# Gathered edges of a graph network: one product per chunk of 128 edges, over 64 destination columns at a fixed place

## The chip, the cores and the metric

One core of one Trainium2 chip runs the whole kernel in one launch. The metric is the device time of one execution in microseconds (us), as the median of the runs shown. Engines are named as the profile names them: PE is TensorE's matmul, PEld its weight load, DVE is VectorE, ACT ScalarE, POOL GpSimd, SP SyncE.

## What is computed

A graph of N = 6250 nodes with D = 128 features and E = 106250 edges, sorted by destination, goes through 14 aggregations one after the other: two SAGE layers, one GCN, two more GCN products, and three layers of three hops each. Each aggregation has the form

```
agg[n] = sum over edges e with dst[e] == n of scale(e) * x[src[e]]        # segment_sum(x[src], dst)
h      = f(agg @ W + x @ W' + b), then a layer norm and a residual in some of them
```

The first five aggregations (the GCN scalings are done on the nodes) sum rows without an edge's weight; the nine hops multiply each row by `edge_weight[e]`.

## The kernel before, in words

Nodes are cut into 49 tiles of 128. An aggregation is a stage `a` (0 to 13), and a stage computes its destination tiles in two ways at once.

**Dense part.** For the later tiles a matrix of edge counts (stages 0 to 4) or edge weights (stages 5 to 13) lies in HBM. SP loads it in units into `room` (6 slots), and `sweep` (L1021) multiplies each of the 49 source tiles with a piece of 512 columns (four destination tiles) into `pwide`.

**Sparse part.** The first 12 tiles (6 pairs; `EARLY`, `FIRST`) or 18 tiles (9 pairs; `LATE`) are done from gathered rows. A pair has `CHP` = 36 chunks of 128 consecutive edges. POOL gathers the source rows of a chunk with one indirect DMA into one of 36 slots of `ring_f` (L628). DVE builds a one-hot of 128 edges by 128 destinations in `hot`, 27 buffers (`one_hot`, L1532 to L1538). PE multiplies the gathered rows by the one-hot into `pstep` (`edges`, L1034 to L1055; the product is L1051). The first 16 chunks of a pair hold only edges of its first tile and those from the 20th on only edges of the second, but chunks 16 to 18 may hold both. So a pair has `STP` = 39 steps for 36 chunks: `step_of` gives for each step the chunk, the side and whether the chunk is new, and the three middle chunks are multiplied twice. `last_step` says which step frees a slot.

Steps go in batches of `HB` = 3 with one semaphore count each (`hot_built`, `batch_done`). All matmuls are f32, and each shows as two weight loads and two passes in the profile. The order on PE is written out by the host: a stage has so many beats, a beat holds the products of 11 of the `sum(dense) * 49` tile pairs (some 2.75 wide products), then the posts (transposes and products with weight matrices) that are due, then the batches that `beat_of` puts there. `lead` beats at the start of a stage (6, 9 in `LATE`, 90 in stage 0) and `trail` beats at its end (8, 4, 2) have no batch.

POOL starts the gathers of stage `a` when all rows of stage `a - 1` are in the table (`rows_out`). Gather `c` waits until the slot's previous chunk has been used (`batch_done`) and, every other chunk, until PE has come to a unit of the sweep (`pace`, at most `AHEAD_UNITS` ahead). In stages 1 to 4 POOL also writes the edge weights of the late matrix with 536 indirect DMAs (`scatter`, L591), spread between the gathers, with some 40 behind the last one.

DVE's work after a group (`post`) is put between the one-hots of the batch that `due` gives, `FH` = 5 batches behind.

**Front.** Before stage 0, DVE sums repeated edges for the scatter lists (`summed`, `place`), counts where tiles begin, decides if the input fits the fast way (`flag`, L1326 to L1336, then `v_flag`), and gives POOL the places of the chunks (`off_i`, L1322, then `off_ready`). Each engine waits for `v_flag` and loads it before its fast part. POOL's fast part first fetches the edge records of the chunks with 21 indirect DMAs (L604: 9 for destinations, 9 for weights, 3 for sources), then scatters 360 and 300 columns of counts (L591), of which each lap waits for the one before to land, and then gathers for stage 0. The counts matrix is zeroed before by ACT's DMA queue (`counts<-zz`); the first scatter waits for 35 of these. DVE's `tables` waits for the 21 fetches, and a walk over 49 tiles of 21 chunks sums the degrees (PE L901, DVE L1370).

Of the kernel before, what the change touches and what calls it, by code (L numbers as in the profile page):

```python
# [10 lines left out]
P = 128  # L11
# [29 lines left out]
STP = 39  # L41
# [3 lines left out]
RB = 3  # L45
HOTS = 27
HB = 3
LEAD, TRAIL = 6, 8
# [9 lines left out]
assert STP % HB == 0 and HOTS % HB == 0 and 2 * MIX + 4 == CHP and CHP + 3 == STP  # L58
KINDS = [0, 1, 2, 3, 4] + ["hop1", "hop2", "hop3"] * LAYERS


def last_step(c):
    return c if c < MIX else 2 * c - MIX + 1 if c < MIX + 3 else c + 3


def step_of(i):
    if i < MIX:
        return i, 0, True
    if i < MIX + 6:
        return MIX + (i - MIX) // 2, (i - MIX) % 2, (i - MIX) % 2 == 0  # L70
    return i - 3, 1, True
# [76 lines left out]
RBLOCKS = -(-((TILES + 1) // 2) // RB)  # L148
WINDOW = 40
# [5 lines left out]
assert SPAN % HB == 0 and SPAN <= HOTS and SPAN >= MIX + 3  # L155
# [3 lines left out]
def pace(a, c):  # L159
    p, (pair, slot) = SPLITS[a], divmod(c, CHP)  # L160
    first = slot if slot < MIX else MIX + 2 * (slot - MIX) if slot < MIX + 3 else slot + 3
    m = p.beat_of((pair * STP + first) // HB) * p.mm // p.beats
# [34 lines left out]
def program(nc, A, out):  # L197
    ctx = ExitStack()
    with ctx:
# [50 lines left out]
        f_dst = sb("f_dst", [P, TILES, SPAN])  # L250
        f_dst_flat = f_dst[:, :, :].rearrange("p t c -> p (t c)")
# [16 lines left out]
        hot = sb("hot", [P, HOTS, P])  # L268
# [89 lines left out]
        v_group = sem("v_group")  # L358
        lanes_in, p_flag, v_flag, lanes_ready, x_copied, kept = names(
# [212 lines left out]
        def _(pool):  # L572
# [8 lines left out]

            def scatter(which, i):
# [12 lines left out]
            def fast():  # L595
                pool.wait_ge(off_ready, 1)
                pool.wait_ge(e_out, 96)
                for k in range(RBLOCKS):
                    n = min(RB * CHP, (PAIRS - 1 - k * RB) * CHP + MIX + 3)
                    for rows_, pad in ((rows_d.bitcast(I32), e_dst), (rows_w, e_wgt), (rows_s.bitcast(I32), e_src)):  # L600
                        if pad is e_src and k * RB >= MOST:
                            continue
                        runs = pad.rearrange("(e a) -> e a", a=1)
                        pool.indirect_dma_start(out=rows_[0:n, k, :], out_offset=None, in_=runs[:, :],  # L604
                                                in_offset=bass.IndirectOffsetOnAxis(ap=off_i[0:n, k:k + 1], axis=0)
                                                ).then_inc(fast_rows, 16)
# [7 lines left out]
                for a, p in enumerate(SPLITS):  # L614
# [253 lines left out]
        def _(pe):  # L868
# [6 lines left out]
            pe.matmul(pstep[1][0:1, 0:1], same[:, 1:2], ones[:, 0:1], start=False, stop=True).then_inc(p_flag, 1)  # L875
            pe.wait_ge(in_w, 16 * (10 + len(ROWS) + 3))
# [5 lines left out]
            def tables_and_degrees():  # L882
                pe.wait_ge(fast_rows, (2 * RBLOCKS + 3) * 16)
# [144 lines left out]
            def selves(a, bank, first, w):  # L1028
                for i in range(w):
                    own = x_of(a)[:, first + i, :]  # L1030
                    ins = pe.matmul(bank[:, i * P:(i + 1) * P], own, ident[:, :], start=False, stop=i == w - 1)
# [786 lines left out]
```

## Time and profile before

| what | value |
| --- | --- |
| median of 3 runs (lowest, highest) | 7283.2 us (7281.24, 7289.38) |
| span of the profiled execution | 7281.5 us |
| PE busy | 6698.5 us, 92% |
| PE weight loads busy | 3984.2 us, 55% |
| POOL busy | 4999.4 us, 69% |
| DVE busy | 2253.5 us, 31% |
| ACT busy | 363.8 us, 5% |
| DMA | 2043.46 MB, mean 281 GB/s |

The page gives the span of the profiled execution and no other time of it. The span is within 0.3 us of the lowest of the three runs. Busy time is the union of the instructions of an engine; POOL's busy time is the part of each indirect DMA in which it writes descriptors, and 0.30 us of issue lie between two of them.

### The profile page before, as it was taken

What the parts mean: (1) busy time and instruction counts of PE and PEld (TensorE: products, weight loads), DVE (VectorE), ACT (ScalarE), POOL (GpSimd) and SP (SyncE); (2) the same over time, 40 slices, a digit from 0 to 9 for tenths busy, and PEclk for the clock granted to TensorE, in tenths of its full rate; (3) what the DMA queues carried; (4) which work ended last, traced back from release to release, by engine and by line L of the source; (5) the groups of instructions that cost most, each with busy time, mean ns of one, the idle gap of its engine ahead of it and who ended that gap; (6) DMA issues with size and microseconds to landing.
All of it is one profiled execution on the core that took longest, in us unless ns stands there. A gap on an engine that the chain in (4) does not pass through costs nothing.

```text
span 7281.5 us, 76418 instructions
## 1 busy us (share of the span) xinstructions
PE 6698.5 (92%) x25545; PEld 3984.2 (55%) x25546; DVE 2253.5 (31%) x8529; ACT 363.8 (5%) x1003; POOL 4999.4 (69%) x5223
## 2 busy tenths in 40 slices
PE   0599749899999999999999999999999999999998
PEld 0599325555555555555555555556555555655555
DVE  8444602222112111222323234322222432322244
ACT  0000000000001000000000000000000000000000
POOL 0677777676666776776767767676776767767676
PEclk9999979999999999999999999999999999999999
DMA  9977738788787887887888888888888888888887
GB/s 363 353 284 292 242 118 281 245 291 295 266 278 258 291 297 276 303 303 258 283 286 284 276 300 279 279 277 283 290 279 293 280 284 278 275 292 285 304 288 236
DMA packets 593113, 2043.46 MB, mean 281 GB/s; under 512 B 135284, under 2 KB 328599, under 8 KB 418780
## 3 DMA queue, kind: packets, MB, share of 16 engines
q1 hardware_dynamic: 309150, 1605.95, 62.3%
q0 software_dynamic: 167184, 263.90, 12.1%
q10 hardware_dynamic: 116428, 169.16, 6.4%
q8 instruction: 193, 3.16, 0.2%
q14 instruction: 158, 1.29, 0.1%
HBM read 1768.09 MB, written 271.72 MB: 280 GB/s over the span
## 4 chain that ended last, share of the span: by engine, by line
PE 66%; DMA 14%; POOL 11%; issue 8%; DVE 0%; POOLq 0%; SPq 0%; ACT 0%; ACTq 0%; DVEq 0%
PE pwide L1021 52%; PE pstep L1051 11%; DMA ring_f<-table,f_src 6%; POOL ring_f L628 5%; DMA counts<-lane_val,lane_idx 4%; POOL counts L591 4%; DMA counts<-zz 3%; POOL weights L591 1%; PE pwide L1105 1%; DMA weights<-lane_val,lane_idx 1%; DMA ring_f<-in_x,f_src 0%; PE pwide L1104 0%; PE pwide L1067 0%; DMA room<-weights 0%; PE pwide L1071 0%
## 5 line engine op out<-in xcount | busy, mean ns | idle before, releaser
L628 POOL DMA_INDIRECT ring_f<-table,f_src x3780 | 3596.2, 951 | 1603.0 <-issue 974.4
L1021 PE MATMUL pwide<-room,hcur 128*128 128x512 f32 (+2 forms) x6076 | 2616.8, 573 | 112.8 <-DMA room<-counts 112.8
L1021 PE MATMUL pwide<-room,acc 128*128 128x512 f32 (+2 forms) x5880 | 2555.4, 575 | 15.2 <-DMA room<-weights 13.5
L1021 PEld LDWEIGHTS pwide<-room,hcur 128*128 128x128 f32 x6076 | 1079.1, 191 | 1106.3 <-issue 1063.3
L1051 PEld LDWEIGHTS pstep<-hot,ring_f 128*128 128x128 f32 x8658 | 1192.2, 192 | 737.9 <-issue 544.9
L1021 PEld LDWEIGHTS pwide<-room,acc 128*128 128x128 f32 x5880 | 1045.7, 191 | 959.6 <-issue 908.4
L1051 PE MATMUL pstep<-hot,ring_f 128*128 128x128 f32 x8658 | 1244.8, 277 | 128.6 <-DMA ring_f<-table,f_src 111.7
L1537 DVE TENSOR_SCALAR hot<-iota,f_dst,f_wgt 128x128 f32<-128x128 f32 x3159 | 892.2, 362 | 1478.0 <-PE pstep L1051 1471.7
L591 POOL DMA_INDIRECT counts<-lane_val,lane_idx x660 | 648.9, 983 | 220.7 <-issue 182.9
L591 POOL DMA_INDIRECT weights<-lane_val,lane_idx x536 | 525.5, 980 | 164.0 <-issue 152.1
L1536 DVE TENSOR_SCALAR hot<-iota,f_dst 128x128 f32<-128x128 f32 x1170 | 260.2, 301 | 811.1 <-PE pstep L1051 806.8
L901 PE MATMUL pstep<-acc,hot 128*128 x2058 | 446.7, 353 | 40.2 <-DVE deg_sums L1375 40.2
L901 PEld LDWEIGHTS pstep<-acc,hot 128*128 128x128 f32 x2058 | 442.7, 332 | 44.2 <-issue 44.2
L1558 DVE SCALAR_TENSOR_TENSOR xres<-pwide,dinv,xres 128x128 f32<-128x128 f32 x294 | 83.3, 344 | 845.3 <-PE pwide L1105 697.4
L628 POOL DMA_INDIRECT ring_f<-in_x,f_src x216 | 204.7, 948 | 65.8 <-issue 60.0
L721 ACT ACTIVATE zz<-pwide 128x512 f32<-128x512 f32 x122 | 70.3, 576 | 3398.3 <-PE pwide L1021 2623.5
L1558 DVE SCALAR_TENSOR_TENSOR zz<-pwide,dinv,xres 128x128 f32<-128x128 f32 x196 | 55.5, 344 | 541.3 <-PE pwide L1105 336.9
L1370 DVE TENSOR_SCALAR hot<-iota,f_dst 128x128 f32<-128x128 f32 x1029 | 208.6, 294 | 2.8
L1105 PEld LDWEIGHTS pwide<-w,zz 128*128 128x128 f32 x882 | 122.4, 192 | 35.6 <-issue 30.6
L604 POOL DMA_INDIRECT ring_f<-e_dst,off_i x9 | 9.3, 1039 | 192.2 <-issue 191.9
L1105 PE MATMUL pwide<-w,zz 128*128 128x128 f32 x882 | 135.2, 275 | 0.6 <-ACT zz L721 0.6
L1558 DVE SCALAR_TENSOR_TENSOR zz<-pwide,rcnt,rows 128x128 f32<-128x128 f32 x49 | 13.9, 344 | 318.6 <-PE pwide L1096 318.6
(261 smaller groups left out, 1674.9 us busy)
## 6 DMA issues: line engine op xcount, KB each, us to landing
room<-weights SPq DMA_DIRECT2D x700, 1024.0 KB
room<-counts SPq DMA_DIRECT2D x540, 1024.0 KB
room<-weights SPq DMA_DIRECT2D x156, 768.0 KB
counts<-zz ACTq DMA_DIRECT2D x64, 1792.0 KB
weights<-zz SPq DMA_DIRECT2D x56, 1792.0 KB
ring_f<-table,f_src POOLq DMA_INDIRECT x3780
room<-weights SPq DMA_DIRECT2D x56, 512.0 KB
room<-counts SPq DMA_DIRECT2D x105, 256.0 KB
```

The lines of the kernel that those rows point to most:

```text
L591: pool.indirect_dma_start(out=m, out_offset=bass.IndirectOffsetOnAxis(ap=lane_idx[which][:, at:at + 1], axis=0), in_=lane_val[which][:, at ...
L604: pool.indirect_dma_start(out=rows_[0:n, k, :], out_offset=None, in_=runs[:, :], in_offset=bass.IndirectOffsetOnAxis(ap=off_i[0:n, k:k + 1 ...
L628: pool.indirect_dma_start(out=ring_f[:, slot, :], out_offset=None, in_=rows_from[:, :], in_offset=bass.IndirectOffsetOnAxis(ap=f_src[:, c: ...
L721: act.activation(zT, bank[:, 0:w * P], ACT.Copy).then_inc(z_done, 1)
L901: ins = pe.matmul(pstep[0][:, 0:2], hot[:, j, :], degree_of[:, bass.ds(it * SPAN + j, 1), :].rearrange("p c a -> p (c a)"), start=j == 0, ...
L1021: ins = pe.matmul(bank[:, 0:w * P], x_of(a)[:, first + o, :], room[:, n % SLOTS, o * w * P:(o + 1) * w * P], start=begins, stop=ends and n ...
L1051: ins = pe.matmul(bank[:, j * P:(j + 1) * P], row, one, start=begins, stop=ends and not own)
L1105: ins = pe.matmul(o, z, w3[:, of + k, :], start=True, stop=True)
L1370: ins = V.tensor_scalar(hot[:, j, :], iota[:, :], f_dst_flat[:, bass.ds(it * SPAN + j, 1)], None, ALU.is_equal)
L1536: return V.tensor_scalar(to, iota[:, :], f_dst[:, 2 * pair + side, col:col + 1], None, ALU.is_equal)
L1537: return V.tensor_scalar(to, iota[:, :], f_dst[:, 2 * pair + side, col:col + 1], f_wgt[:, pair * CHP + c:pair * CHP + c + 1], ALU.is_equal ...
L1558: ins = V.scalar_tensor_tensor(to[:, j, :], po[:, j, :], scale_of(kind)[:, first + j:first + j + 1], more(j), ALU.mult, ALU.add)
```

## The change

1. A pair has 36 steps for 36 chunks (`STP = CHP`). Chunk `c` is multiplied once, by a one-hot of `WIN` = 64 columns that begin at `LOWS[c]` within the 256 columns of the pair (0 for the first chunks, then 7 or 8 further each, 192 for the last). `step_of` and `last_step` are gone. The product goes to `bank[:, low:low + 64]`, which may lie across two tiles and begins at any column.
2. DVE compares 64 numbers with `f_win[:, pair, c]`, the destination minus the pair's first node minus `LOWS[c]`. `tables` builds `f_win` with nine more operations. The buffers are halves of the old ones; `hot` has 21 of 128 columns in place of 27.
3. A check on the chip: for the first and last destination of each chunk of the nine pairs, DVE compares with the window; PE sums over the partitions, and the flag is multiplied by the result. For this POOL's fetches move ahead of the flag, and the destinations of the first three blocks come first, with a semaphore of their own. The flag now waits until those have landed.
4. A test that the first tile of a gathered pair has 16 full chunks is gone; 36 small memsets on POOL write `LOWS` at the start.

The number of gathers, the gathered bytes, the dense part, `lead` and `trail` stay.

```diff
-STP = 39
+STP = CHP
+WIN = 64
+LOWS = [min(max((15 * c - 56) >> 1, 0), 2 * P - WIN) for c in range(CHP)]
...
-        hot = sb("hot", [P, HOTS, P])
+        hot = sb("hot", [P, SPAN, P])
+        windows = hot[:, :, :].rearrange("p s (h d) -> p (s h) d", d=WIN)
...
+            for c in range(CHP):
+                pool.memset(lows[:, :, c:c + 1], float(LOWS[c])).then_inc(g_lows, 1)
+
+            pool.wait_ge(off_ready, 1)
+            pool.wait_ge(e_out, 96)
+            blocks = [(k, rows_d.bitcast(I32), e_dst) for k in range(RBLOCKS)]
+            blocks += [(k, rows_w, e_wgt) for k in range(RBLOCKS)] + [(k, rows_s.bitcast(I32), e_src) for k in range(WBLOCKS)]
+            for k, rows_, pad in blocks:
...
+                                        ).then_inc(window_rows if pad is e_dst and k < WBLOCKS else fast_rows, 16)
...
-                            freed = (PAIR0[a] + pair - 1) * STP + last_step(slot)
+                            freed = (PAIR0[a] + pair - 1) * STP + slot
...
+            pe.wait_ge(v_unfit, 1)
+            pe.matmul(pstep[1][0:1, 1:2], outside[:, :], ones[:, 0:1], start=True, stop=True).then_inc(p_unfit, 1)
...
-                c, side, fresh = step_of(i)
...
-                j = 2 * pair + side - first
+                low = (2 * pair - first) * P + LOWS[i]
...
-                if fresh:
-                    pe.wait_ge(chunk_in[c], (PAIR0[a] + pair + 1) * 16)
-                one, row = hot[:, ((BATCH0[a] + batch) * HB + n) % HOTS, :], ring_f[:, c, :]
-                ins = pe.matmul(bank[:, j * P:(j + 1) * P], row, one, start=begins, stop=ends and not own)
+                pe.wait_ge(chunk_in[i], (PAIR0[a] + pair + 1) * 16)
+                one, row = windows[:, ((BATCH0[a] + batch) * HB + n) % HOTS, :], ring_f[:, i, :]
+                ins = pe.matmul(bank[:, low:low + WIN], row, one, start=begins, stop=ends and not own, skip_group_check=True)
...
+            dve.wait_ge(window_rows, WBLOCKS * 16)
+            edges = RB * CHP
+            link(V.tensor_copy(low_at[0:edges, 5, :], rows_d[0:edges, 0:WBLOCKS, 0].bitcast(I32)))
+            link(V.tensor_copy(low_at[0:edges, 6, :], rows_d[0:edges, 0:WBLOCKS, P - 1].bitcast(I32)))
+            link(V.tensor_tensor(unfit[0:edges, :], low_at[0:edges, 5, :], low_at[0:edges, 3, :], ALU.is_lt))
...
+            link(V.reduce_sum(outside[0:edges, :], unfit[0:edges, :], axis=mybir.AxisListType.X))
+            dve.sem_inc(v_unfit, 1)
...
+            dve.wait_ge(p_unfit, 1)
+            link(V.tensor_scalar(flag[:, 2:3], pstep[1][0:1, 1:2], 0.5, None, ALU.is_lt))
+            link(V.tensor_tensor(flag[:, 0:1], flag[:, 0:1], flag[:, 2:3], ALU.mult))
...
+                    if side == 0 and p < MOST:
+                        ins = V.scalar_tensor_tensor(f_win[:, p, :], pwide[:, at:at + CHP], float(t * P), lows[:, 0, :],
+                                                     ALU.subtract, ALU.subtract)
...
-                pair, i = divmod(s, STP)
-                c, side, _ = step_of(i)
-                col, to = c - WALK * side, hot[:, (BATCH0[a] * HB + s) % HOTS, :]
+                pair, c = divmod(s, CHP)
+                to, at = windows[:, (BATCH0[a] * HB + s) % HOTS, :], f_win[:, pair, c:c + 1]
                 if a < STAGES:
-                    return V.tensor_scalar(to, iota[:, :], f_dst[:, 2 * pair + side, col:col + 1], None, ALU.is_equal)
+                    return V.tensor_scalar(to, iota[:, 0:WIN], at, None, ALU.is_equal)
```

## Rows read from the trace of the kernel before

**Rows 1.** The page's first lines: span, busy shares, granted TensorE clock in 40 slices

```profile
span 7281.5 us, 76418 instructions
...
PE 6698.5 (92%) x25545; PEld 3984.2 (55%) x25546; DVE 2253.5 (31%) x8529; ACT 363.8 (5%) x1003; POOL 4999.4 (69%) x5223
...
PEclk9999979999999999999999999999999999999999
```

**Rows 2.** By stage from gather start to gather start: stage 1, 5 (hop 1), 6 (hop 2)

```profile
core 0: us, PE busy (x) PEld busy (x) DVE busy (x) ACT busy (x) POOL busy (x), PEclk, DMA share, GB/s
1396.10:1878.30 482.20, 473.05 (x1691) 259.55 (x1692) 116.04 (x482) 33.30 (x88) 338.42 (x350) 0.99 0.81 277
...
3341.50:3778.20 436.70, 431.47 (x1763) 256.52 (x1762) 121.80 (x412) 27.49 (x75) 306.67 (x324) 1.00 0.82 280
3778.20:4213.30 435.10, 425.81 (x1638) 244.90 (x1637) 121.54 (x415) 21.49 (x62) 308.60 (x324) 1.00 0.85 286
```

**Rows 3.** Gathers alone (L628), first to last of a stage: stages 5 and 10

```profile
3341.50:3746.90 405.40, 306.67 (x324) 1.00 0.82 278
...
5531.10:5938.20 407.10, 308.45 (x324) 1.00 0.84 282
```

**Rows 4.** POOL in order of time, the first gather of stage 2

```profile
1878.40 0.98 POOL L628 DMA_INDIRECT ring_f<-table,f_src  x1 [15.88 <-DMA table<-hcur]
```

**Rows 5.** PE in order of time behind the last gathers of stages 5 and 10

```profile
3754.26 2.10 PE L1021 MATMUL pwide<-room,acc 128*128 128x384 f32 x6
...
5939.22 0.49 PE L1051 MATMUL pstep<-hot,ring_f 128*128 128x128 f32 x2 [0.43 <-DMA ring_f<-table,f_src]
...
5942.80 2.42 PE L1021 MATMUL pwide<-room,hcur 128*128 128x384 f32 x7
```

**Rows 6.** PE in order of time in stage 4, products of 128 columns between wide ones

```profile
3002.69 1.05 PE L1100 MATMUL pwide<-w,zz 128*128 128x128 f32 x8
3003.58 2.74 PE L1021 MATMUL pwide<-room,hcur 128*128 128x512 f32 x6
3006.16 0.83 PE L1051 MATMUL pstep<-hot,ring_f 128*128 128x128 f32 x6
3006.82 2.74 PE L1021 MATMUL pwide<-room,hcur 128*128 128x512 f32 x6
```

**Rows 7.** PE in order of time, four products of 64 columns (L1065) before wide ones

```profile
1924.22 1.00 PE L1065 MATMUL pwide<-wc,zz 128*128 128x64 f32 x8
1925.06 2.79 PE L1021 MATMUL pwide<-room,hcur 128*128 128x512 f32 x6
1927.69 0.60 PE L1078 MATMUL pwide<-ident,zz 128*64 128x128 f32 x4
```

**Rows 8.** POOL in order of time in the front: first and last fetch, first scatter

```profile
192.48 1.17 POOL L604 DMA_INDIRECT ring_f<-e_dst,off_i  x1 [189.75 <-issue]
...
219.67 1.11 POOL L604 DMA_INDIRECT ring_f<-e_wgt,off_i  x1 [0.30 <-issue]
221.09 1.00 POOL L591 DMA_INDIRECT counts<-lane_val,lane_idx  x1 [0.30 <-issue]
```

**Rows 9.** DVE in order of time in the front: chunk places, then the flag

```profile
186.86 0.17 DVE L1322 CAST off_i<-off_f 128x9 int32<-128x9 f32 x1
...
190.18 0.14 DVE L1336 CAST flag_i<-flag 1x1 int32<-1x1 f32 x1
```

**Rows 10.** The fetches of L604: from issue to landing

```profile
DMA to landing us min/median/max: 7.7/9.5/19.1
```

**Rows 11.** The chain in order of time: the zeroing that ends before the scatters

```profile
195.52 10.73 DMA counts<-zz
```

**Rows 12.** PE groups by shape: edges; the degree walk; the first 128-column transposes

```profile
L1051 PE MATMUL pstep<-hot,ring_f 128*128 128x128 f32 x8658 | 1244.8, 277 | 128.6 <-DMA ring_f<-table,f_src 111.7 <-DMA ring_f<-in_x,f_src 15.3
L901 PE MATMUL pstep<-acc,hot 128*128 x2058 | 446.7, 353 | 40.2 <-DVE deg_sums L1375 40.2
...
L878 PE MATMUL pstep<-ident,room 128*128 128x128 f32 x4 | 1.1, 431 | 0.0
```

More of the change, by code:

```diff
@@ L57 @@
 FH = 5
-assert STP % HB == 0 and HOTS % HB == 0 and 2 * MIX + 4 == CHP and CHP + 3 == STP
+assert STP % HB == 0 and HOTS % HB == 0 and 2 * MIX + 4 == CHP
 KINDS = [0, 1, 2, 3, 4] + ["hop1", "hop2", "hop3"] * LAYERS
[L62 to L71, printed above, removed]
 class Split:
@@ L148 @@
 RBLOCKS = -(-((TILES + 1) // 2) // RB)
+WBLOCKS = -(-MOST // RB)
 WINDOW = 40
@@ L154 @@
 WB = SPAN // HB
-assert SPAN % HB == 0 and SPAN <= HOTS and SPAN >= MIX + 3
+assert SPAN % HB == 0 and HOTS * WIN <= SPAN * P and SPAN >= MIX + 3 and SPAN >= BODY
 AHEAD_UNITS = 6
 def pace(a, c):
-    p, (pair, slot) = SPLITS[a], divmod(c, CHP)
-    first = slot if slot < MIX else MIX + 2 * (slot - MIX) if slot < MIX + 3 else slot + 3
-    m = p.beat_of((pair * STP + first) // HB) * p.mm // p.beats
+    p = SPLITS[a]
+    m = p.beat_of(c // HB) * p.mm // p.beats
     k, m = divmod(m, 4 * TILES)
@@ L250, in program @@
         f_dst = sb("f_dst", [P, TILES, SPAN])
+        f_win = sb("f_win", [P, MOST, CHP])
+        lows = sb("lows", [P, 1, CHP])
+        low_at = sb("low_at", [P, 8, WBLOCKS])
+        low_i = sb("low_i", [P, 1], I32)
+        unfit = sb("unfit", [P, WBLOCKS])
+        outside = sb("outside", [P, 1])
         f_dst_flat = f_dst[:, :, :].rearrange("p t c -> p (t c)")
@@ L580, in _ @@
                                pattern=[[-1, P]], channel_multiplier=1).then_inc(g_const, 1)
+            for c in range(CHP):
[5 more added lines that the diff above has]
+            for k, rows_, pad in blocks:
+                n = min(RB * CHP, (PAIRS - 1 - k * RB) * CHP + MIX + 3)
+                runs = pad.rearrange("(e a) -> e a", a=1)
+                pool.indirect_dma_start(out=rows_[0:n, k, :], out_offset=None, in_=runs[:, :],
+                                        in_offset=bass.IndirectOffsetOnAxis(ap=off_i[0:n, k:k + 1], axis=0)
+                                        ).then_inc(window_rows if pad is e_dst and k < WBLOCKS else fast_rows, 16)
             def scatter(which, i):
@@ L595, in fast @@
             def fast():
[L596 to L606, printed above, removed]
                 for which in range(2):
@@ L1026, in sweep, with selves @@
                     ins.then_inc(unit_used, 1)
-            def selves(a, bank, first, w):
+            def selves(a, bank, first, w, shared=False):
                 for i in range(w):
                     own = x_of(a)[:, first + i, :]
-                    ins = pe.matmul(bank[:, i * P:(i + 1) * P], own, ident[:, :], start=False, stop=i == w - 1)
+                    ins = pe.matmul(bank[:, i * P:(i + 1) * P], own, ident[:, :], start=False, stop=i == w - 1,
+                                    skip_group_check=shared)
                 return ins
@@ L1047, in edges @@
                     pe.wait_ge(z_done, GROUP0[b] + SPLITS[b].rank[1, qb] + 1)
-                if fresh:
-                    pe.wait_ge(chunk_in[c], (PAIR0[a] + pair + 1) * 16)
-                one, row = hot[:, ((BATCH0[a] + batch) * HB + n) % HOTS, :], ring_f[:, c, :]
-                ins = pe.matmul(bank[:, j * P:(j + 1) * P], row, one, start=begins, stop=ends and not own)
+                pe.wait_ge(chunk_in[i], (PAIR0[a] + pair + 1) * 16)
+                one, row = windows[:, ((BATCH0[a] + batch) * HB + n) % HOTS, :], ring_f[:, i, :]
+                ins = pe.matmul(bank[:, low:low + WIN], row, one, start=begins, stop=ends and not own, skip_group_check=True)
                 if ends and own:
-                    ins = selves(a, bank, first, w)
+                    ins = selves(a, bank, first, w, True)
                 if n == HB - 1:
@@ L1380, in general @@
             def general():
+                dve.wait_ge(fast_rows, 2 * RBLOCKS * 16)
                 V.memset(snat_i, 0)
@@ L1531, in one_hot @@
             def one_hot(a, s):
[L1532 to L1534 removed]
+                pair, c = divmod(s, CHP)
+                to, at = windows[:, (BATCH0[a] * HB + s) % HOTS, :], f_win[:, pair, c:c + 1]
                 if a < STAGES:
[L1536 to L1537 removed]
+                    return V.tensor_scalar(to, iota[:, 0:WIN], at, None, ALU.is_equal)
+                return V.tensor_scalar(to, iota[:, 0:WIN], at, f_wgt[:, pair * CHP + c:pair * CHP + c + 1],
                                        ALU.is_equal, ALU.mult)
```

26 lines of the change are left out of this document (22 added, 4 removed).

## The prediction

> **What bounds the kernel now.** I read the page first. PE is busy for 92% of the span and POOL for 69% [rows 1]. That invites "PE is the bound", but the stages differ, so I cut the span at the first gather of each stage.
>
> Stage 1 (sparse part of 6 pairs) lasts 482.2 us. PE is busy for 473.1 of it, and the idle 9.1 us lie at its head, where the first gathers have yet to land. POOL writes 350 descriptor sets of 0.97 us with 0.30 us between, 443.4 us in all, so it waits for 38.8 us [rows 2]. The last of these waits, 15.9 us, is for the table's rows [rows 4]. PE sets the length of such a stage.
>
> Stage 5 (9 pairs) lasts 436.7 us, stage 6 lasts 435.1 [rows 2]. Here POOL gathers without a pause: 324 gathers in 405.4 us, 1.251 us each, and the rest, 31 us, is the way from the last gather to complete rows in the table. PE is idle for 5.2 and 9.3 us. The nine late stages are a loop through POOL. In stages like 6 and 10 PE waits for gathers until near the end (0.43 us at 5939.22), and is through with its last batch at 5942.8, 4.6 us after the last gather at 5938.2 [rows 3, 5]. In the three first hops (5, 8, 11), which have more posts on PE, it is behind: 3754.3 against 3746.9, 7.4 us [rows 3, 5]. Stage 0 is a loop through POOL too: scatters from 221.1 [rows 8], then 216 gathers, back to back.
>
> **What an edge step costs.** A batch of three steps of 128 columns takes 0.66 us, from 3006.16 to 3006.82: 0.111 us a pass, 0.222 a step [rows 6]. For 64 columns there is a direct row, a product with a 64-column weight matrix. Its eight passes take 0.84 us, from 1924.22 to 1925.06; eight of 128 columns take 0.89. But the six wide passes behind the narrow ones take 2.63 us (1925.06 to 1927.69), and behind the 128-column ones 2.58 (3003.58 to 3006.16). Together 3.47 and 3.47 us [rows 6, 7]. Narrowing a product from 128 to 64 columns is worth nothing here: something that each pass pays whatever its columns, by all appearance the load of 128 x 128 weights, sets the pitch. I take 0. The bounds: half of a pass, 0.056 us, gained; or up to the 0.217 us of the degree walk's passes (446.7 us for 2058), the farthest row, lost [rows 12].
>
> The Trainium skill, "TensorE: Matmul & The Clock Gate", section "LDWEIGHTS (loading the stationary operand)", gives the load by its 128 columns alone, some 107 ns, and the trace's 0.111 us agrees. Its section "Back-to-back issue gap" gives an isolated matmul a gap by its own columns; by that rule alone half the columns would halve the pass, which is the third rival below.
>
> **The change, part by part.**
>
> *Steps.* A pair loses 3 of 39 steps: 18 in each stage of 6 pairs, 27 in each of 9. That is 4.0 and 6.0 us of PE, 5 x 18 + 9 x 27 = 333 steps or 74 us in all. What it is worth depends on the loop.
> - Stages 1 to 4: PE is the bound, and nothing hidden comes up, since POOL has 15.9 us at the end of a stage to give: 4 x 4.0 = **16 us**.
> - Stages 5, 8, 11: PE can catch up only until it waits for gathers, from 7.4 to about 4.9 us behind them, 2.5 us each: **7.5 us**. Bounds 0 and 6 us each.
> - Stages 6, 7, 9, 10, 12, 13: PE already runs at the gathers' heels. The 6 us become idle time: **0**. Bounds 0 and 6 each.
> - Stage 0: POOL's gathers end it: **0** (up to 4).
>
> *One-hots.* DVE's get narrower and fewer. DVE is busy for 31% [rows 1] and waits for free buffers. 27 buffers of 64 columns stay 27. Worth 0, hidden by PE's work. POOL's 1.251 us a gather (1.257 in stage 10) I take as fixed; a change of 0.01 us in it would be 3 us a late stage [rows 3].
>
> *Order.* `beat_of` spreads 108 batches over the beats of 117 (72 over 78), the same first and last beats, so the slots come free at about the same times. DVE's posts stay 5 batches behind, far from its end. 0.
>
> *Front.* Today the chunk places are there at 187.0, the flag at 190.3, and POOL begins its fetches at 192.48, 2.1 us behind the flag; the first scatter is at 221.09, so 21 fetches take 28.6 us [rows 8, 9]. After: POOL begins at some 187.4 and is through at 216.0; then it loads the flag (2.1 us) and scatters from 218.1. The zeroing that it needs ends at 206.3 [rows 11]. The flag must be there by 216. The third fetch of destinations is issued at 187.4 + 2 x 1.36 = 190.1 and lands 9.5 us later, 199.6; then some 13 chained DVE operations of 0.19 us (today 17 take the 3.3 us from 186.86 to 190.18 [rows 9]), one tiny product on PE, and the old 3.3 us of flag operations with two more: about 206. Ten us to spare; with the longest landing, 19.1 us [rows 10], it would be 216, just in time. The scatters and gathers up to stage 1 are one chain on POOL, so all of it moves: **3 us gained**. Bounds: 5 gained, 5 lost. Queued behind DVE's new wait are the flag and `place(1)`, whose list POOL needs 360 scatters later, and then `tables`, which waits for the fetches anyway. The 36 memsets of POOL lie in its idle 190 us. The nine operations in `tables` are ahead of the degree walk, whose end PE and stage 0 don't wait for last.
>
> Sum: 16 + 7.5 + 3 = 26.5 us. The profiled span of 7281.5 becomes 7255; the median of the runs, 1.7 us above the span, 7283.2, becomes **7256.7**, say 7256. A measurement of this kernel can tell about 0.2%, 14.6 us, from no change; the forecast is 0.37%.
>
> **Rivals.**
>
> *B, PE is the bound everywhere.* PE's 92% and its 5 to 9 us of idle time in a late stage speak for it. Then all 74 us and the 3 of the front count: 7283.2 - 77 = 7206. Against it: 324 gathers with no wait for a slot, in every late stage [rows 3].
>
> *C, the gain is taken over by POOL.* In stages 1 to 4 POOL's own time is 443 us of 482, scatters wait for landings, and a shorter stage may leave POOL behind, or the flag may come late by a few us. Then little but the first hops is left, 5 to 8 us: 7277. For it: POOL's waits of 38.8 us in stage 1 are partly for its own landings. Against: 15.9 us of them are not.
>
> *D, narrow passes run in half the time.* 7992 passes x 0.056 = 447 us of PE. POOL caps it: the late stages give no more than above, a stage like 1 ends at 443 us plus its head of 16 and some 8 us of landings, about 18 us less: 72 + 7.5 + 3, so 7283 - 83 = 7200. Against it: rows 7.
>
> *E, slower: the edge passes fall to half speed.* The first 128-column transposes took 431 ns in place of 275, and the degree walk's two-column passes 217 ns each although PE looked fully busy; the page still shows a granted clock of 0.9 or more there [rows 1, 12]. If narrow columns bring edges to that price, they cost 7992 x 0.217 = 1734 us in place of 8658 x 0.111 = 961: 773 us more, less the late stages' idle time of some 9 x 9 and what the missing steps give, about 7970. It decides from 961 / 7992 = 0.120 us a pass on. Against it: wide passes fill four fifths of a stage (in stage 6 the edges' 702 passes of 0.111 us are 78 of 426 us), and rows 7 show no such price.
>
> The Trainium skill, same page, Part 1 on the clock gate, says that the clock is throttled by default and that activity releases it; by it, work with fewer columns could lose the 2.4 GHz level for 1.2. The late stages are granted 1.00 [rows 2], and by that rule too I see no fall.
>
> That the change doesn't take effect is a small part of E: were a chunk outside its window, the flag would send all engines to the general program. Counted from the reference's inputs, the 324 chunks of the nine pairs lie inside by 21 columns or more.
>
> **Chances.** Forecast 0.66, B 0.10, C 0.13, D 0.05, E 0.06. B, D and the forecast are faster by over 0.2%: 0.81. C is the same: 0.13. Slower: 0.06. The forecast alone, with its bounds on front and first hops and a little from the other hops, is 7240 to 7270. The range reaches to B below and to C above and leaves D and E out: 7204 to 7277.
>
> **What would show it.** In the changed profile: L1051's successor with 7992 passes at a pitch of 0.111 us; stages 1 to 4 shorter by 4 us each; gathers of 405 us in the late stages, and stages 6, 7, 9, 10 and 12 as long as before, with some 6 us more idle time on PE; stages 5, 8, 11 shorter by 2 to 3 us, the last batch some 5 us behind the last gather; first fetch at 187, first scatter at 218, flag near 206. A late stage shorter by 6 us would prove B right; a batch of three steps under 0.5 us without longer wide passes, D; the first scatter behind 221, a misread front.

## The result, and the profile of the changed kernel

The changed kernel takes 7250.3 us (median of 4 runs, 7247.3 to 7260.8), the kernel before 7285.0 in the same comparison (4 runs, 7281.2 to 7289.4). The ratio is 0.9955, 95% interval 0.994 to 0.9971: 0.45% faster, 32.8 us. The forecast was 7256, 0.37% faster. The profiled execution took 7249.3 us for a span of 7247.4, so 1.9 us lie around the span.

The page, first lines and three groups (columns: line, engine, operation, tiles, shape, count, then busy us and mean ns of one, then idle time before and its releaser):

```profile
span 7247.4 us, 74832 instructions
...
PE 6643.0 (92%) x24881; PEld 3922.3 (54%) x24882; DVE 2046.5 (28%) x8231; ACT 363.8 (5%) x1003; POOL 4992.3 (69%) x5259
...
L1053 PE MATMUL pstep<-hot,ring_f 128*128 128x64 f32 x7992 | 1084.6, 268 | 152.7 <-DMA ring_f<-table,f_src 133.4
...
L1571 DVE TENSOR_SCALAR hot<-iota,f_win,f_wgt 128x64 f32<-128x64 f32 x2916 | 734.0, 336 | 1540.8 <-PE pstep L1053 1534.3
```

The successor of the old edge product is L1053, with the 7992 passes that the prediction named. PE is busy for 55.5 us less than in [rows 1], DVE for 207, and POOL, which has the same gathers to issue, for 7 us less. The time fell by less than PE's work did.

The windows from first gather to first gather of stages 1, 5 and 6, then the gathers alone of stages 5 and 10 (columns as in [rows 2]; the header says them again):

```profile
core 0: us, PE busy (x) PEld busy (x) DVE busy (x) ACT busy (x) POOL busy (x), PEclk, DMA share, GB/s
1400.10:1878.00 477.90, 470.09 (x1657) 255.41 (x1657) 105.16 (x464) 33.29 (x88) 339.12 (x351) 0.99 0.81 281
3326.60:3763.10 436.50, 428.90 (x1712) 252.17 (x1711) 104.12 (x386) 27.48 (x75) 306.26 (x324) 1.00 0.83 282
3763.10:4195.10 432.00, 419.57 (x1579) 238.84 (x1578) 104.03 (x386) 21.48 (x62) 306.60 (x325) 1.00 0.85 287
...
3326.50:3731.40 404.90, 306.27 (x324) 1.00 0.83 280
...
5504.20:5910.10 405.90, 307.19 (x324) 1.00 0.84 283
```

Stage 1 fell from 482.2 to 477.9. The gathers alone take 404.9 and 405.9 us where [rows 3] has 405.4 and 407.1. In stage 6 PE has 12.4 us of idle time, before it had 9.3 [rows 2]: its work fell by 6.2 us, the stage by 3.1.

The table cuts every profiled execution at the first gather of each stage (us). "Others late" are stages 6, 7, 9, 10 and 12. One row is one execution, and the two executions of the kernel before show how far such a number wanders by itself.

| kernel | first gather | stage 0 | stages 1 to 4 | first hops 5, 8, 11 | others late | 13 to end |
| --- | --- | --- | --- | --- | --- | --- |
| before | 1090.6 | 305.6 | 1945.4 | 1312.6 | 2189.1 | 438.0 |
| before, again | 1091.0 | 305.6 | 1945.2 | 1313.7 | 2182.3 | 438.7 |
| changed | 1090.4 | 309.7 | 1926.5 | 1307.6 | 2176.4 | 436.8 |
| w128 | 1087.8 | 307.3 | 1927.1 | 1306.0 | 2182.5 | 437.4 |
| s39 | 1085.7 | 304.2 | 1950.7 | 1310.9 | 2181.4 | 436.6 |
| s39e | 1090.4 | 304.5 | 1949.7 | 1305.0 | 2183.0 | 437.9 |
| s39l | 1082.4 | 308.0 | 1924.1 | 1316.6 | 2181.4 | 435.3 |
| first39 | 1089.2 | 304.3 | 1923.9 | 1306.4 | 2183.4 | 436.3 |
| half | 1082.4 | 307.7 | 1934.4 | 1306.9 | 2181.3 | 435.5 |
| frontold | 1091.5 | 313.2 | 1922.0 | 1309.9 | 2181.4 | 437.5 |
| g33 | 1091.5 | 309.4 | 1924.0 | 1284.2 | 2079.7 | 420.0 |
| trail2 | 1087.0 | 312.8 | 1926.2 | 1287.0 | 2175.9 | 437.6 |
| best | 1084.3 | 305.5 | 1898.7 | 1291.8 | 2184.2 | 436.2 |

And the times, each beside the kernel before of its own comparison:

| run | median us | ratio to before, 95% interval |
| --- | --- | --- |
| w128 | 7252.4 | 0.9963 (0.9949 to 0.9977) |
| s39 | 7271.5 | 0.9987 (0.9978 to 0.9996) |
| s39e | 7267.0 | 0.9978 (0.9966 to 0.9989) |
| s39l | 7251.2 | 0.9962 (0.9949 to 0.9976) |
| half | 7250.1 | 0.9952 (0.9937 to 0.9967) |
| frontold | 7257.5 | 0.9962 (0.9949 to 0.9976) |
| g33 | 7101.0 | 0.9748 (0.9735 to 0.9762) |
| trail2 | 7230.1 | 0.9925 (0.9912 to 0.9939) |
| first39 | 7243.3 | 0.9952 (0.9938 to 0.9966) |
| before, again | 7284.8 | 1.0007 (0.9998 to 1.0016) |
| best | 7201.4 | 0.9892 (0.9877 to 0.9907) |

The first four were compared with 7280.0 us, the next four with 7283.5, the last three with 7281.2. Between comparisons, then, a difference of 3 us is nothing.

### The profile page after: what moved, and what is told of

Its sections match the earlier page's. It is cut to its first block, busy times and chain, and to the rows that moved or that the text cites. A ratio compares the mean times of both kernels' runs of the same rounds, so it can differ in the third digit from the quotient of the medians.

```text
span 7247.4 us, 74832 instructions
## 1 busy us (share of the span) xinstructions
PE 6643.0 (92%) x24881; PEld 3922.3 (54%) x24882; DVE 2046.5 (28%) x8231; ACT 363.8 (5%) x1003; POOL 4992.3 (69%) x5259
## 4 chain that ended last, share of the span: by engine, by line
PE 62%; DMA 14%; POOL 12%; issue 9%; DVE 1%; SPq 1%; POOLq 0%; ACT 0%; ACTq 0%; DVEq 0%
PE pwide L1024 50%; PE pstep L1053 9%; POOL ring_f L629 7%; DMA ring_f<-table,f_src 7%; DMA counts<-lane_val,lane_idx 4%; POOL counts L603 4%; DMA weights<-lane_val,lane_idx 1%; POOL weights L603 1%; PE pwide L1107 1%; SPq L468 1%; DMA ring_f<-in_x,f_src 1%; PE pwide L1106 0%; PE pwide L1069 0%; DMA first_dst<-in_dst 0%; PE pwide L1073 0%
## 5 line engine op out<-in xcount | busy, mean ns | idle before, releaser
L1024 PE MATMUL pwide<-room,hcur 128*128 128x512 f32 (+2 forms) x6076 | 2653.6, 581 | 116.4 <-DMA room<-counts 115.0
L1024 PE MATMUL pwide<-room,acc 128*128 128x512 f32 (+2 forms) x5880 | 2589.2, 583 | 14.3 <-DMA room<-weights 11.2
L1053 PEld LDWEIGHTS pstep<-hot,ring_f 128*128 128x128 f32 x7992 | 1105.2, 192 | 713.4 <-issue 522.4
L1053 PE MATMUL pstep<-hot,ring_f 128*128 128x64 f32 x7992 | 1084.6, 268 | 152.7 <-DMA ring_f<-table,f_src 133.4
L1571 DVE TENSOR_SCALAR hot<-iota,f_win,f_wgt 128x64 f32<-128x64 f32 x2916 | 734.0, 336 | 1540.8 <-PE pstep L1053 1534.3
L1570 DVE TENSOR_SCALAR hot<-iota,f_win 128x64 f32<-128x64 f32 x1080 | 205.5, 274 | 799.0 <-PE pstep L1053 794.7
L1592 DVE SCALAR_TENSOR_TENSOR zz<-pwide,dinv,xres 128x128 f32<-128x128 f32 x196 | 55.5, 345 | 580.3 <-PE pwide L1107 371.9
L1404 DVE TENSOR_SCALAR hot<-iota,f_dst 128x128 f32<-128x128 f32 x1029 | 209.1, 296 | 2.8
```

Of the source, the lines that this page charges most:

```text
L1024: ins = pe.matmul(bank[:, 0:w * P], x_of(a)[:, first + o, :], room[:, n % SLOTS, o * w * P:(o + 1) * w * P], start=begins, stop=ends and n ...
L1053: ins = pe.matmul(bank[:, low:low + WIN], row, one, start=begins, stop=ends and not own, skip_group_check=True)
L1404: ins = V.tensor_scalar(hot[:, j, :], iota[:, :], f_dst_flat[:, bass.ds(it * SPAN + j, 1)], None, ALU.is_equal)
L1570: return V.tensor_scalar(to, iota[:, 0:WIN], at, None, ALU.is_equal)
L1571: return V.tensor_scalar(to, iota[:, 0:WIN], at, f_wgt[:, pair * CHP + c:pair * CHP + c + 1], ALU.is_equal, ALU.mult)
L1592: ins = V.scalar_tensor_tensor(to[:, j, :], po[:, j, :], scale_of(kind)[:, first + j:first + j + 1], more(j), ALU.mult, ALU.add)
```

## The experiments

### Are the columns worth anything? w128

Every chunk once, as in the changed kernel, but with 128 columns from the same place.

```diff
-HOTS = 27
-WIN = 64
+HOTS = 24
+WIN = 128
...
-        hot = sb("hot", [P, SPAN, P])
+        hot = sb("hot", [P, HOTS, P])
```

> The changed kernel with one-hots of 128 columns in place of 64 (24 buffers for 27, since 27 don't fit); still 36 steps a pair. Theory (each pass pays the load of 128 weights, the columns are free): the same time as the changed kernel, 7250 us within 5, and stages 1 to 4 as long as there. Rival (narrowing brings a part of the 34 us): slower than 7260, and a batch of three with the wide passes behind it longer.

Measured: 7252.4 us, the ratio within 0.0008 of the changed kernel's. PE's timeline around two batches of stage 4, first of the changed kernel, then of w128 (columns: start us, us of the group, engine, line, tiles, shape, passes; the ends of groups are modelled and overlap, so the pitch is read from start to start):

```profile
3006.82 2.74 PE L1024 MATMUL pwide<-room,hcur 128*128 128x512 f32 x6
3009.40 0.78 PE L1053 MATMUL pstep<-hot,ring_f 128*128 128x64 f32 x6
3010.01 4.51 PE L1024 MATMUL pwide<-room,hcur 128*128 128x512 f32 x10
3014.36 0.78 PE L1053 MATMUL pstep<-hot,ring_f 128*128 128x64 f32 x6
```

```profile
3004.45 0.83 PE L1053 MATMUL pstep<-hot,ring_f 128*128 128x128 f32 x6
3005.12 4.46 PE L1024 MATMUL pwide<-room,hcur 128*128 128x512 f32 x10
3009.41 0.83 PE L1053 MATMUL pstep<-hot,ring_f 128*128 128x128 f32 x6
```

The batch of 64 columns takes 0.61 us, the one of 128 takes 0.67; the ten wide passes behind them take 4.35 and 4.29. Batch and wide passes together are 4.96 us both times. It is the same exchange as in [rows 6, 7]: the narrow product ends 0.06 us early, and the product behind it gives it back. Narrowing is worth 0 in time. That one product covers both tiles doesn't come from the 64 columns either: it comes from where the columns begin, and w128 places 128 of them across the two tiles in the same way. What 64 columns save is room for buffers, 27 in place of w128's 24.

### What are the steps worth, and where? s39, s39e, s39l, first39

The changed kernel with the old count of 39 steps a pair: chunks 16 to 18 are multiplied a second time, with one-hots that are all zeros. s39 does so in every stage, s39e in stages 0 to 4, s39l in stages 5 to 13, first39 in stage 0 alone.

```diff
-STP = CHP
+STP_EARLY, STP_LATE = 39, 39
...
-                pair, i = divmod(batch * HB + n, STP)
+                pair, i = divmod(batch * HB + n, p.stp)
+                c, again = step_of(p, i)
...
-                pe.wait_ge(chunk_in[i], (PAIR0[a] + pair + 1) * 16)
+                if not again:
+                    pe.wait_ge(chunk_in[c], (PAIR0[a] + pair + 1) * 16)
```

> The changed kernel with 39 steps a pair again: chunks 16 to 18 are multiplied a second time by a one-hot of zeros, 64 columns wide. Theory (the missing steps brought nearly all): back to 7280 us, 7274 to 7287. Rival (narrowing, or the front, brought it): stays below 7265.

> 39 steps a pair in stages 0 to 4 only, 36 in the late ones. Theory (PE sets the length of stages 1 to 4): 16 to 20 us above the changed kernel, 7268, in stages 1 to 4. Rival C (POOL sets them): within 5 us of it.

> 39 steps a pair in the nine late stages only, 36 in stages 0 to 4. Theory (POOL sets them): 8 to 19 us above the changed kernel, 7258 to 7269, PE's idle time some 5 us less in each. Rival B (PE sets them): 27 steps x 0.222 x 9 = 54 us above, 7304.

Measured, by ratio against the changed kernel's 0.9955: s39 is 0.0032 above it, some 23 us, where the three terms of the prediction for steps add up to 16 + 7.5 + 0 = 23.5. That the two are so close is partly luck: in the table s39 has 24.2 us more in stages 1 to 4, 3.3 in the first hops and 5.0 in the other late stages, and 5.5 less in stage 0. s39e has 90 of the 333 steps, 20 us of PE, and is 0.0023 above, 17 us. This too is a balance: its stages 1 to 4 are 23.2 us longer, for 72 steps or 16 us of PE, and its stage 0 is 5.2 us shorter. In stages 1 to 4 all of PE's work counts. Rival C, by which POOL takes the gain back, is refuted by the table: there the four profiles with 39 steps have 1945.2 to 1950.7 us, the seven with 36 steps and the same `lead` and columns of weights 1922.0 to 1927.1. s39l has 243 of the 333 steps, 54 us of PE, and is 0.0007 above, 5 us, not told from zero by the interval. Stage 6 of s39l:

```profile
3752.70:4186.00 433.30, 425.24 (x1639) 245.12 (x1638) 110.30 (x416) 21.49 (x62) 307.10 (x325) 1.00 0.84 288
```

PE has 60 passes more than in the changed kernel's stage 6 and is busy for 5.7 us more; the stage is 1.3 us longer. So rival B, by which those 54 us would all count, is refuted by a run. In the first hops s39l is 9.0 us above the changed kernel, 3.0 a stage; its other late stages are 5.0 above it, but level with first39, half and w128, which have 36 steps.

Stage 0 speaks against the prediction. The five executions with 39 steps there (before twice, s39, s39e, first39) have 304.2 to 305.6 us; the seven with 36 steps and the same lead of 90 beats have 307.3 to 313.2, mean 309.7. first39 was built for this:

> 39 steps a pair, three of them with a one-hot of zeros, in stage 0 alone. Theory (stage 0 got longer in the changed kernel, 309.7 us from first gather to first gather in place of 305.6, since PE waits longer for its gathers there and its clock falls; with the old steps it keeps busy): stage 0 at 304 to 306 us and the time 3 to 5 us below the changed kernel's, in spite of 18 more products. Rival (stage 0's 4 us are chance between executions): 307 to 311 us, no gain.

It took stage 0 back to 304.3 us. Its median, 7243.3, lies below the changed kernel's, but the two ratios, 0.9952 and 0.9955, don't differ beyond their intervals: the 5 us are read from the table, not from the total. PE's timeline of the changed kernel near the end of stage 0, and the granted clock of that stretch (columns of the window as above):

```profile
1356.49 0.44 PE L1053 MATMUL pstep<-hot,ring_f 128*128 128x64 f32 x2 [2.46 <-DMA ring_f<-in_x,f_src]
1356.77 4.18 PE L1024 MATMUL pwide<-room,hcur 128*128 128x128 f32 x22
...
1355.00:1362.00 7.00, 5.50 (x35) 5.51 (x35) 0.00 (x0) 0.45 (x1) 3.83 (x5) 0.76 0.52 143
```

The same place in the kernel before, and in first39:

```profile
1356.41 2.62 PE L1021 MATMUL pwide<-room,hcur 128*128 128x128 f32 x22
...
1355.00:1362.00 7.00, 6.57 (x59) 6.38 (x59) 0.00 (x0) 0.60 (x1) 4.62 (x5) 1.00 0.77 215
```

```profile
1354.12 2.67 PE L1042 MATMUL pwide<-room,hcur 128*128 128x128 f32 x22
```

With 36 steps PE comes to a chunk before it has landed and waits for 2.46 us. Behind this wait the clock is granted at 0.76 on average, so part of the stretch is at the 1.2 GHz level, and 22 passes take 4.18 us in place of 2.62. PE then reaches the last batch late: edges end 7.0 us behind the last gather, where the kernel before needs 4.2. The Trainium skill, "TensorE: Matmul & The Clock Gate", Part 1 ("What's actually happening"), has it that the throttled state is the default and that activity releases it; the trace agrees in its direction, 2.62 against 4.18 us.

It happens a second time, some 8 us behind the last batch, after a wait for a unit of the sweep:

```profile
1375.09 4.33 PE L1024 MATMUL pwide<-room,acc 128*128 128x512 f32 x6 [2.86 <-DMA room<-counts]
```

In the kernel before these six passes take 2.81 us behind a wait of 1.37. So 1.5 us are the longer wait and 1.5 the slower passes, and from the end of the last batch to the last write of rows to the table there are now 28.3 us, where there were 25.3. In all 2.8 and 3.0 us are lost, and 1.7 came back in the gathers and in the way from that write to the next gather. A PE with less to do waited, ran slower behind the waits, and came late to the one place where it was waited for.

first39 takes away both the waits and the new order of batches. s39l tells them apart: its stage 0 has 36 steps in the changed kernel's order, but near the end of that stage PE happened to wait for 1.69 us at most and kept its clock (columns of the window as above):

```profile
1340.00:1387.00 47.00, 39.63 (x214) 27.39 (x212) 6.51 (x25) 4.51 (x9) 9.41 (x10) 1.00 0.83 309
```

Its edges end 4.4 us behind the last gather and its last write follows 25.4 us later, as with 39 steps. So the late batch and the late write come with the longer waits and the lower clock behind them, and not with the order. Its stage 0 was long even so, 308.0 us, because 8.5 us passed between that write and the next stage's first gather, where the other profiles have 3.4 to 6.9: this part varies by itself, and a stage 0 of one profile isn't explained by waits and clock alone.

### Is a pass's pitch set by the load? half

```diff
-                ins = pe.matmul(bank[:, low:low + WIN], row, one, ...)
+                ins = pe.matmul(bank[0:64, low:low + WIN], row[:, 0:64], one, ...)
```

Half of each product is left out, so the result is not the right one; two memsets (not shown) zero `pstep` first.

> Leaves out half of the work of the edge products: of each gathered row only the first 64 features are the loaded weights, so that a load has 64 columns and a pass has 64; the gathers stay whole. Theory (the load sets the pitch): a pass of the edges at 0.056 us in place of 0.111, stages 1 to 4 shorter until POOL sets them (up to some 20 us each), late stages as in the changed kernel or some 2 us shorter: 7165 to 7210. Rival (something else per pass sets the pitch): pitch stays 0.111, time stays 7250.

Measured: 7250.1 us. The time that was expected didn't come. PE in stage 4:

```profile
3002.36 2.74 PE L1024 MATMUL pwide<-room,hcur 128*128 128x512 f32 x6
3005.04 0.56 PE L1053 MATMUL pstep<-hot,ring_f 128*64 128x64 f32 x6
3005.53 4.56 PE L1024 MATMUL pwide<-room,hcur 128*128 128x512 f32 x10
3010.02 0.56 PE L1053 MATMUL pstep<-hot,ring_f 128*64 128x64 f32 x6
```

Inside a batch the starts of passes are 0.058 us apart, where they are 0.111 with 128-column loads and the same 64 moving columns (in the changed kernel's trace five such passes span 0.67 us and six 0.78). With w128, where 128 moving columns left the pitch at 0.111, this answers what sets it: the load does. The Trainium skill, same page, section "LDWEIGHTS (loading the stationary operand)", makes the load proportional to its columns, and this run agrees with it, 0.058 against 0.111 us.

But the batch as a whole takes 0.49 us, not 6 x 0.058 = 0.35; the six wide passes ahead of it take 2.68 in place of 2.58, and the ten behind it 4.49 in place of 4.35. Batch and ten wide passes are 4.98 us, as before the edit. At each change between 128 and 64 weight columns some 0.1 us is lost, and stages 1 to 4 came out 8 us longer. The likely reason is that a load isn't begun under the passes ahead of it when the shape changes (weight loads are idle for 0.76 us ahead of such a batch, against 0.24 without the change of shape); this was only read from the trace.

### What is the front worth? frontold

The windows' check is taken out and the fetches stand behind the flag again, in the old order; all else is as in the changed kernel.

```diff
-            for k, rows_, pad in blocks:
...
+                pool.wait_ge(off_ready, 1)
+                pool.wait_ge(e_out, 96)
+                for k in range(RBLOCKS):
...
-            dve.wait_ge(window_rows, WBLOCKS * 16)
...
-            dve.wait_ge(p_unfit, 1)
```

> The changed kernel without the check of the windows, and POOL's 21 fetches behind the flag and in the old order again. Theory (the front is worth 0 to 3 us): first scatter some 3 us later, time within 5 us of the changed kernel. Rival (the new order in the front costs what stage 0 lost): 5 us or more faster.

Measured: 7257.5 us, 0.0007 above the changed kernel, 5 us with an interval that holds 0. POOL of the changed kernel at its first fetch and first scatter, and DVE at the window rows and the flag (columns: start, us, engine, line, in brackets the idle time before and its releaser):

```profile
189.45 1.16 POOL L590 DMA_INDIRECT ring_f<-e_dst,off_i  x1 [185.52 <-DVEq L1324]
...
217.52 1.11 POOL L603 DMA_INDIRECT counts<-lane_val,lane_idx  x1 [0.30 <-issue]
```

```profile
202.10 0.30 DVE L1340 CAST low_at<-ring_f 108x3 f32<-108x3 int32 x1 [10.14 <-DMA ring_f<-e_dst,off_i]
...
208.26 0.14 DVE L1366 CAST flag_i<-flag 1x1 int32<-1x1 f32 x1
```

The first scatter is 3.6 us earlier than in [rows 8], as forecast, and the flag is there 9 us before POOL needs it. Yet the first gather of stage 0 came at 1090.4, level with 1090.6. POOL's waits between 217 and 1090 us (columns: us, number, longest), before and changed:

```profile
POOL counts L591 <- DMA counts<-lane_val,lane_idx: 37.8, 70, 10.7
```

```profile
POOL counts L603 <- DMA counts<-lane_val,lane_idx: 46.4, 79, 10.4
```

In this execution the scatters waited 8.6 us longer for their own landings. Over all profiles such waits scatter: the first gather lies between 1082.4 and 1091.5 us in the ten executions with the new front, mean 1087.1, and between 1090.6 and 1091.5 in the three with the old one. The front is worth some 4 us on average. That its gain is missing from the profiled pair is, by this spread, chance.

### What bounds the late stages? g33 and trail2

g33 leaves 3 of 36 gathers of a pair out, in the late stages alone.

```diff
-                        pool.indirect_dma_start(out=ring_f[:, slot, :], ...
+                        if a < STAGES or slot % 12 != 11:
+                            pool.indirect_dma_start(out=ring_f[:, slot, :], ...
...
-                pe.wait_ge(chunk_in[i], (PAIR0[a] + pair + 1) * 16)
+                if a < STAGES or i % 12 != 11:
+                    pe.wait_ge(chunk_in[i], (PAIR0[a] + pair + 1) * 16)
```

> Leaves out 3 of the 36 gathers of each pair in the nine late stages (slots 11, 23 and 35 keep old rows; every product is still made). Theory (POOL sets the late stages): each shorter by PE's idle time there, 7 to 18 us, in all 60 to 110 us: 7140 to 7190. Rival B (PE sets them): within 5 us of the changed kernel.

Measured: 7101.0 us, 0.0207 below the changed kernel, 151 us; 60 to 110 had been expected. Stage 6 of g33:

```profile
3750.70:4168.60 417.90, 417.90 (x1588) 238.51 (x1587) 103.53 (x387) 21.54 (x62) 282.50 (x298) 1.00 0.87 295
```

POOL has 27 gathers fewer, 27 x 1.25 = 34 us, and the stage is 14.1 us shorter, down to PE's own busy time: no idle time is left. PE now is some 20 us behind the last gather. With PE's work untouched stages 6, 7, 9, 10, 12 and 13 fell by 14 to 25 us each; with PE's work raised by 6 us each (s39l) they hardly moved. Gathers are their bound. The first hops, where PE is closer to being the bound, fell by 5 to 11 us. The estimate was too low for two reasons: over the nine late stages PE is idle for 121 us in the changed kernel and for 28 in g33, so there was more idle time to win than was put down, and PE's busy time fell by some 44 us too, with no pass left out. What made it fall wasn't looked into.

The rest of a late stage, 32 us in stage 5 and 27 in stage 6 of the changed kernel, lies behind the last gather. trail2 takes two of the four beats that the host holds back behind the last batch:

```diff
-LATE = Split([4, 4, 4, 4, 2], [4] * 7 + [3], 9, 4)
+LATE = Split([4, 4, 4, 4, 2], [4] * 7 + [3], 9, 2)
```

> The changed kernel with trail 2 in place of 4 in the late stages: the last batches two beats later, with nothing else changed. Theory (in the late stages the way from the last gather to complete rows is part of the loop, and PE has idle time to spend): the last group's rows come one beat of 2.4 us sooner behind the last gather, 10 to 20 us faster, 7230 to 7240. Rival (the last beats are not in the loop): 7250 within 5.

Measured: 7230.1 us, 0.003 below the changed kernel, some 20 us, as forecast in sum. But not by stage: the first hops gave 20.6, the other late stages 0.5. Stage 5:

```profile
3326.00:3754.20 428.20, 424.21 (x1705) 250.45 (x1704) 100.88 (x374) 27.50 (x75) 306.10 (x324) 1.00 0.84 285
```

It is 8.3 us shorter than the changed kernel's. From the end of the last batch to the next stage's first gather stage 5 needs 18.5 us in place of 25.9, stage 6 needs 22.0 in place of 23.9. The later batches do the same in both: the last write to the table comes 2.0 us sooner behind the last batch. What differs is the time from this write to the next stage's first gather. In the first hops it fell from 8.8, 8.2 and 7.9 us to 3.2, 3.8 and 3.1, in the others it didn't, and in stage 12 it rose from 5.1 to 9.2. Why wasn't found.

### The kernel before once more, and a faster one: beforecopy, best

> The kernel before once more, for a second profile: how far one profile of a stage can be trusted. Ratio 1.000 within 0.2%. If the six late stages of hop 2 and 3 were shorter in the changed kernel for a reason other than chance (5 of them: 2176 us against 2189), they take 2185 to 2192 us here; if by chance, 2177 to 2184.

Measured: 7284.8 us, ratio 1.0007 (0.9998 to 1.0016). Its other late stages sum up to 2182.3 us where the first profile has 2189.1: 6.8 us apart with no edit between them. This is the measure for every number of the table.

best is the changed kernel with fewer beats without batches:

```diff
-FIRST = Split([4, 4, 4], [4] * 9 + [1], 90, 2)
-EARLY = Split([4, 4, 4], [4] * 9 + [1])
-LATE = Split([4, 4, 4, 4, 2], [4] * 7 + [3], 9, 4)
+FIRST = Split([4, 4, 4], [4] * 9 + [1], 92, 0)
+EARLY = Split([4, 4, 4], [4] * 9 + [1], 9)
+LATE = Split([4, 4, 4, 4, 2], [4] * 7 + [3], 9, 2)
```

> The changed kernel with the batches placed by what binds each stage: trail 2 in the late stages (as in trail2, which gave 20 us), lead 9 in place of 6 in stages 1 to 4, where PE waits 5 to 8 us at the head for the first gathers, and lead 92, trail 0 in stage 0, whose gathers end it. Theory: 20 us from the late stages, 3 to 6 us in each of stages 1 to 4, 0 to 5 in stage 0: 7200 to 7220. Rival (a later first batch only moves the wait to the end of the stage): 7225 to 7235.

Measured: 7201.4 us (7199.4 to 7203.4), ratio 0.9892 (0.9877 to 0.9907), faster than both kernels. Stages 1 and 2:

```profile
1389.80:1861.90 472.10, 462.72 (x1641) 251.84 (x1640) 104.27 (x464) 33.29 (x88) 339.94 (x350) 0.99 0.82 283
1861.90:2353.30 491.40, 487.11 (x1764) 266.18 (x1764) 90.19 (x415) 45.87 (x137) 339.20 (x351) 1.00 0.81 280
```

Against the changed kernel stages 1 to 4 gave 27.8 us, the first hops 15.8, stage 0 gave 4.2. In stage 1 PE is busy for 462.7 of 472.1 us, against 470.1 of 477.9: batches begin three beats later there and the gathers have more of a start, but both busy and idle time changed, and which of the edits gave what in stages 0 to 4 wasn't run apart.

## Why the prediction was right

**Steps, stages 1 to 4: 16 us.** Right in mechanism, and near in sum. The pair gives 18.9, s39e, which brings the steps back, is 23.2 us longer there, and the profiles with 36 steps have 1922.0 to 1927.1 (half and best left out). PE was the bound, and POOL's slack held: it waits for 19.8 us before the first gather of stage 2, where it waited for 15.9. The split is not the forecast one. Each stage was to give 4; in the pair stages 1 to 4 gave 4.3, 0.6, 6.2 and 7.8, and why isn't known.

**Steps, first hops: 7.5 us.** Right in kind; the term was a little large. The pair gives 5.0; the mean over the four executions with 39 steps (before twice, s39, s39l) is 1313.5 us, over the five plain ones with 36 (changed, w128, s39e, first39, frontold) 1307.0, so 6.5. As the prediction has it, PE could catch up only to the gathers: in stage 5 the last batch is done 5.6 us behind the last gather (3736.99 on this line, less 3731.4), against 7.4 in [rows 3, 5].

```profile
3736.99 2.15 PE L1024 MATMUL pwide<-room,acc 128*128 128x384 f32 x6
```

**Steps, other late stages: 0.** The pair shows 12.7 us less, as if this were wrong. It is mostly chance: with 39 steps the mean of four executions is 2183.6 us, with 36 (the five above and half) 2181.3. Some 2 us are left for five stages, less than the spread of either group, and s39l and g33 name the bound, POOL's gathers.

**Steps, stage 0: 0, up to 4 gained.** This step failed: 5 us lost. It took in that POOL's gathers end the stage and that PE would idle, and not that the clock can fall behind a longer wait and make PE late there. Its bounds had no loss in them.

**Narrowing: 0.** Right. w128 has the same time, and half shows what sets the pitch. The whole gain in the stages is that of 36 products for 39. Rival D falls with it.

**One-hots, order: 0.** No stage shows a price. DVE still waits for PE to free its buffers, for 1534 us at L1571.

**Front: 3 us.** Right in size over many executions (4), absent in the profiled pair. The first fetch came at 189.45, not 187.4, since the places were ready 2 us later than before; from there to the first scatter are 28.1 us, of which 0.30 lie between the last fetch and the scatter. So the flag's load, for which 2.1 us had been put down, doesn't show, and the scatter at 217.5 was half a microsecond ahead of forecast. The flag was at 208.3 for a forecast of 206, with the window rows waited for until 202.1 and not 199.6.

**Rivals.** B would have made s39l some 54 us slower than the changed kernel: 5 were seen. C had POOL take the gain back: stages 1 to 4 kept theirs. E needed 0.120 us a pass from narrow columns: a batch of 0.61 us over 6 passes is 0.102. What was real of it, a lost clock, came in behind a wait for a gather in stage 0.

**The sum.** In the profiled pair the span fell by 34.1 us: 0.2 in the front, -4.1 in stage 0, 18.9 in stages 1 to 4, 5.0 in the first hops, 12.7 in the other late stages, 1.2 at the end. The forecast had 3, 0, 16, 7.5, 0 and 0. So the total was nearer than its terms, and the largest deviation, 12.7 for 0, is the one that the repeated profiles show as chance for the most part.

Open: s39 and s39e, which do the old number of steps, have 1950 us in stages 1 to 4 where the kernel before has 1945. Why stages with repeated steps cost 5 us more than the old ones wasn't found.

## What to carry to other kernels

Cut the span at the places where one stage hands over to the next and ask in each what ended it: of 74 us of PE work that were removed, some 23 counted, and these were where PE had the last word. Work taken from an engine that isn't the bound can cost time, where the engine then waits and is late at the end of the stage; and the beats that a written-out order holds back at both ends of a stage are worth trying again after such an edit (46 us more here by the ratios, on an edit of 33). When an edit does two things at once, as here fewer products and narrower ones, run each alone: the narrower ones were worth nothing. And profile one kernel twice before a difference of a few microseconds in some stages gets a cause: five stages together moved by 6.8 us by themselves.

## What the runs showed of the hardware

**The clock shown before its first record.** The degree walk from 250 to 700 us in the profiles of the changed kernel and of trail2, which has the same code there (columns of windows; the clock is the third number from the end):

```profile
250.00:700.00 450.00, 419.96 (x1935) 416.24 (x1935) 207.70 (x1032) 1.28 (x1) 343.27 (x351) 1.00 0.76 301
```

```profile
250.00:700.00 450.00, 420.52 (x1938) 416.80 (x1938) 207.71 (x1029) 1.28 (x1) 343.14 (x351) 0.50 0.76 300
```

The busy time is the same, the granted clock 1.00 and 0.50. Since the passes take the same 353 ns on average, the walk runs at the 1.2 GHz level in both, and the 1.00 is what stands there when no change of the clock has been recorded yet: trail2's profile has a fall at 243 us, the changed kernel's has no entry before 743. The prediction's rival E wondered at slow passes under a full clock [rows 12]; the clock wasn't full.

**A short wait can cost clock, but need not.** Waits of PE of 2.46 and 2.86 us were followed by passes at the lower level: 22 passes in 4.18 us against 2.62, and six wide ones in 4.33 against 2.81. In stage 7 of the same profile a wait of 2.95 us was not: the granted clock from 4288 to 4298 us is 1.00, and from the first of the six wide passes behind the wait to the next group are 2.64 us.

```profile
4291.09 0.44 PE L1053 MATMUL pstep<-hot,ring_f 128*128 128x64 f32 x2 [2.95 <-DMA ring_f<-table,f_src]
4291.36 2.79 PE L1024 MATMUL pwide<-room,acc 128*128 128x512 f32 x6
```

**The pitch of narrow passes goes with the columns of their loads.** Passes of 64 moving columns start 0.111 us apart behind loads of 128 columns and 0.058 behind loads of 64; 128 moving columns behind loads of 128 take 0.111 too.

**A change of weight width costs.** Some 0.1 us at each switch between loads of 128 and of 64 columns, which took back all that the shorter loads gave.
